# The causal mask of the transposed attention scores, added by VectorE in PSUM in place of a product with the identity on TensorE

## What is computed

```
mod = silu(c) @ wmod                      # six rows of 1024 per batch: sa, ca, ga, sb, cb, gb
h = layernorm(x) * (1 + ca) + sa
q, k, v = rope(h @ Wq), rope(h @ Wk), h @ Wv     # 32 query heads, 8 key/value heads, 32 wide
att = q . k / sqrt(32), -inf where key > query   # causal
x = x + ga * ((softmax(att) @ v) @ Wo)
h = layernorm(x) * (1 + cb) + sb
x = x + gb * (h @ W.T + bias + lora(h))
```

## Time and profile before

| what | us |
|---|---|
| median of 3 runs (2609.54 to 2612.29) | 2611.24 |
| profiled execution | 2611.64 |
| its span, first to last instruction | 2609.9 |
| PE busy / PEld busy | 2514.4 (96%) / 1871.7 (72%) |
| POOL busy | 1649.7 (63%) |
| DVE busy | 1577.4 (60%) |
| ACT busy | 1021.0 (39%) |
| granted TensorE clock, mean of the span | 0.973 |

### The profile page before, as it was taken

How to read it: one execution, slowest core, us unless ns; L and a number is a source line. 1 busy time by engine, 2 the same in 40 slices (tenths; PEclk the granted TensorE clock), 3 DMA queues, 4 the chain that set the end, 5 groups by cost and what they waited for, 6 DMA issues and landing times. The chain is left out here.

```text
span 2609.9 us, 37478 instructions
## 1 busy us (share of the span) xinstructions
PE 2514.4 (96%) x14476; PEld 1871.7 (72%) x14476; DVE 1577.4 (60%) x2509; ACT 1021.0 (39%) x1301; POOL 1649.7 (63%) x863
## 2 busy tenths in 40 slices
PE   5999999996999999999999999899899999999998
PEld 2788888885766666666666666565588788888886
DVE  4667666655766666666666666465755455454553
ACT  3333333321455665565555666465411111111110
POOL 4543333331488898988988889787555455555553
PEclk8999999997799999999999999899999999999999
DMA  7432233325324335225332335230433433333330
GB/s 277 137 114 103 99 114 113 113 89 173 95 74 131 79 81 139 76 67 144 83 91 53 71 81 161 56 79 19 161 97 97 111 91 97 108 95 105 113 89 25
DMA packets 179726, 267.53 MB, mean 103 GB/s; under 512 B 20508, under 2 KB 113884, under 8 KB 178400
## 3 DMA queue, kind: packets, MB, share of 16 engines
q1 hardware_dynamic: 179552, 265.13, 34.5%
HBM read 183.22 MB, written 80.81 MB: 101 GB/s over the span
## 5 line engine op out<-in xcount | busy, mean ns | idle before, releaser
L927 POOL TENSOR_TENSOR p_sum<-p_sum,p_ring 128x1024 f32<-128x1024 f32 (+2 forms) x465 | 993.9, 2171 | 188.5 <-PE ctx_ps L997 170.4
L850 DVE TENSOR_REDUCE neg_max<-scores_q 128x1 f32<-128x512 f32 (+3 forms) x1216 | 740.6, 658 | 390.8 <-PE scores_q L983 226.5
L792 ACT ACTIVATE p_ring<-scores 128x1024 f32<-128x1024 f32 (+2 forms) x512 | 463.6, 918 | 250.4 <-PE scores L965 178.9
L979 PE MATMUL scores_q<-k_stack,q_stack 96*128 96x512 f32 (+3 forms) x1536 | 467.5, 381 | 0.4 <-DVE prefetched L892 0.4
L961 PE MATMUL scores<-q_stack,k_stack 98*128 98x512 f32 (+1 forms) x1216 | 417.4, 421 | 12.7 <-ACT p_ring L792 11.8
L469 POOL TENSOR_TENSOR roped_hilo<-roped_hilo 128x512 fp32r<-128x512 f32 x80 | 104.3, 1304 | 333.2 <-ACT roped_hilo L329 333.2
L961 PEld LDWEIGHTS scores<-q_stack,k_stack 98*128 98x128 f32 x1216 | 195.5, 192 | 166.1 <-issue 96.2
L979 PEld LDWEIGHTS scores_q<-k_stack,q_stack 96*128 96x128 f32 x1536 | 284.7, 198 | 38.1 <-DVE neg_max L850 4.2
L512 PE MATMUL proj_ps<-h_hi,w_hi 128*128 128x512 f32 x768 | 304.6, 397 | 1.6 <-POOL h_lo L462 1.6
L512 PE MATMUL proj_ps<-h_hi,w_lo 128*128 128x512 f32 x768 | 300.2, 391 | 0.0
L512 PE MATMUL proj_ps<-h_lo,w_hi 128*128 128x512 f32 x768 | 300.0, 391 | 0.0
(11 more groups left out here) (147 smaller groups left out, 3722.3 us busy)
## 6 DMA issues: line engine op xcount, KB each, us to landing
q_stack<-qk_t SPq DMA_DIRECT2D x96, 512.0 KB, 6.9
qk_t<-roped_hilo SPq DMA_DIRECT2D x80, 512.0 KB, 2.7
x_in<-in_L_attn_resid SPq DMA_DIRECT2D x32, 512.0 KB, 6.3
prefetched<-in_L_wmod SPq DMA_DIRECT2D x4, 4096.0 KB, 13.9
ctx_t<-ctx_raw SPq DMA_DIRECT2D x64, 256.0 KB, 4.5
prefetched<-ctx_t SPq DMA_DIRECT2D x31, 512.0 KB, 4.1
prefetched<-inv_t SPq DMA_DIRECT2D x124, 128.0 KB, 5.4
k_stack<-qk_t SPq DMA_DIRECT2D x96, 128.0 KB, 8.8
```

The source lines that it names most:

```text
L792: nc.scalar.activation(probs(n, u), src, ACT.Exp, scale=SM_SCALE).then_inc(s_ex.sem, 1)
L850: nc.vector.tensor_reduce(negm[:, lo // HALF, hs[0]:hs[-1] + 1, i:i + 1], src, AX.X, ALU.max, negate=True).then_inc(s_mx.sem, 1)
L927: nc.gpsimd.tensor_tensor(a, a, probs(n, u), ALU.add).then_inc(s_ap.sem, 1)
L979: last = nc.tensor.matmul(dst[:, a, :], qs[0:MHI, n % QS, h, i * P:(i + 1) * P], ks[0:MHI, n % QS, lo:lo + w], start=not first, stop=not d ...
```

## The change

The mask products on PE go, with the table `mask_k_q` and its four copies on ACT. In their place DVE adds the mask (third part of `consts`, in SBUF, repeated over the heads) to the first 128 columns of each head of a diagonal unit, in place in PSUM (`mask_diagonal`), at the step "scores" of its list: behind the maxima of the steps before it. The exponential of a diagonal unit waits for that add (`diagonal_masked`) instead of the scores; the others wait for the scores as before. The wait of PE and DVE at the start of the stage counts four copies fewer.

```diff
+DIAGONAL = [u for u in range(NE) if EXP_UNITS[u][3] == P * EXP_UNITS[u][1]]
+ND = len(DIAGONAL)
...
-        maskT = sb("mask_k_q", [P, G, P], F32R)
...
+        def scores_of(n, u):
+
+            w, t = EXP_UNITS[u][4], sc[(NE * n + u) % SS]
+            return (t[:, :].rearrange("p (h n) -> p h n", h=2)[:, :, 0:w] if w > 256
+                    else t[:, 0:G * w].rearrange("p (h n) -> p h n", h=G))
...
             def exp(n, u):
                 hf, j, hs, lo, w = EXP_UNITS[u]
-                act.wait_ge(s_p2.sem, s_p2.at(NE * n + u + 1))
+                if u in DIAGONAL:
+                    act.wait_ge(s_dm.sem, s_dm.at(ND * n + DIAGONAL.index(u) + 1))
+                else:
+                    act.wait_ge(s_p2.sem, s_p2.at(NE * n + u + 1))
...
+            def mask_diagonal(n, u):
+                at, heads = scores_of(n, u)[:, :, 0:P], len(EXP_UNITS[u][2])
+                dve.wait_ge(s_p2.sem, s_p2.at(NE * n + u + 1))
+                nc.vector.tensor_tensor(at, at, consts[:, 2 * P:3 * P].rearrange("p (a n) -> p a n", a=1).broadcast_to([P, heads, P]),
+                                        ALU.add).then_inc(s_dm.sem, 1)
...
-                if kind == "mod":
+                if kind == "scores" and step[2] in DIAGONAL:
+                    mask_diagonal(n, step[2])
+                elif kind == "mod":
...
-                                            qs[0:KS, n % QS, h0:h0 + per, lo:lo + w], start=True, stop=not diag)
-                if diag:
-                    for a in range(len(hs) // per):
-                        last = nc.tensor.matmul(o[a][:, :, 0:P], identr[:, :], maskT[:, 0:per, :], start=False, stop=True)
+                                            qs[0:KS, n % QS, h0:h0 + per, lo:lo + w], start=True, stop=True)
                 last.then_inc(s_p2.sem, 1)
```

More of the change, by code:

```diff
@@ L595, in attention @@
         s_mr = [count(f"max_stacked{i}", 32) for i in range(QS)]
-        s_p2, s_ex, s_pv = count("exp_scores"), count("probs_ready"), count("values_done")
+        s_p2, s_ex, s_pv, s_dm = count("exp_scores"), count("probs_ready"), count("values_done"), count("diagonal_masked")
         s_av, s_ap = count("probs_added_dve"), count("probs_added_pool")
@@ L770, in _ @@
                 nc.scalar.activation(maskS[:, h, :], consts[:, P:2 * P], ACT.Copy).then_inc(init.sem, 1)
-                nc.scalar.activation(maskT[:, h, :], consts[:, 2 * P:3 * P], ACT.Copy).then_inc(init.sem, 1)
             def exp(n, u):
                 hf, j, hs, lo, w = EXP_UNITS[u]
-                act.wait_ge(s_p2.sem, s_p2.at(NE * n + u + 1))
+                if u in DIAGONAL:
+                    act.wait_ge(s_dm.sem, s_dm.at(ND * n + DIAGONAL.index(u) + 1))
+                else:
+                    act.wait_ge(s_p2.sem, s_p2.at(NE * n + u + 1))
                 if j == 0:
@@ L788, in exp @@
                             act.wait_ge(s_ap.sem, s_ap.at(NP * before[0] + POOL_ADDS.index(before[1]) + 1))
[L789 to L792, removed]
+                nc.scalar.activation(probs(n, u), scores_of(n, u), ACT.Exp, scale=SM_SCALE).then_inc(s_ex.sem, 1)
             def take_ctx(n, hf):
@@ L841, in _ @@
             nc.vector.memset(negm[:, 1, :, 0:WIDE[0]], LARGE).then_inc(init.sem, 1)
-            dve.wait_ge(init.sem, 2 * G + 5)
+            dve.wait_ge(init.sem, G + 5)
             def take_max(n, m):
@@ L945, in _ @@
         def _(pe):
-            pe.wait_ge(init.sem, 2 * G + 5)
+            pe.wait_ge(init.sem, G + 5)
             def scores(n, u):
@@ L954, in scores @@
                     pe.wait_ge(s_ex.sem, s_ex.at(at - SS + 1))
-                diag = lo == P * j
                 per = 1 if w > 256 else HALF // w
```

## The result

The changed kernel takes 2575.71 us (median of 4 runs, 2574.49 to 2579.28) against 2611.76 before (4 runs, 2609.54 to 2613.45): ratio 0.9865, 95% interval 0.9848 to 0.9882. The forecast was 2580, the range 2551 to 2614.

What follows compares the result with a forecast made beforehand. PE was taken as the bound at 35.48 us a group; minus 2.32 removed, plus stalls of 0.56 and 0.68, gives 34.40. 31 × 1.08 saved less 2 in the last group: 2611.6 − 31.5 = 2580 us, range 2551 to 2614.

Steps and rivals of the forecast that it cites:

- PE is the bound before: Ordinary attention group: PE issues without a pause and sets the 35.48 us period; POOL is second, 3.4 us short of it.
- Removed: 2.32 us: PE, per group: dropping 22 mask products saves 2.32 us by their starts, so PE alone would need 33.16 us.
- the 2.2 below which the prediction called itself wrong: Sign of error: PE's starts next to the removed products move by less than 2.2 us per group.
- Price of the add: VectorE: 12 mask adds per group, eight at 0.43 and four at 0.69 us, 6.2 us in all.
- The walk, 0.56 + 0.68 = 1.24: Units 2 to 5 and 16 to 19 traced: PE stalls 0.56 us at unit 5 and 0.68 at units 18 and 19.
- Hidden: POOL and the copy of the maxima: Per group: POOL's adds have 1.99 us of slack; the maxima copy lands 0.4 us before the next unit 0; neither cuts in.
- POOL's floor: POOL's adds keep the period from going under 33.54 us; rival with POOL setting the pace: 2553 us, chance 0.17.
- Last group, +2 (0 to 5): Last attention group: masks may queue behind 15 VectorE adds, one or two waits costing 2 us, 0 to 5.
- The sum, 33.5 saved and 2 given back: Whole kernel: 31 groups at 1.08 us save 33.5, the last group gives back 2, leaving 31.5 saved.
- The rival "slower": VectorE's queue takes PE's place: 0.1 us more per mask costs 0.5 us a group; 2637 us at 0.8; chance 0.15.

Runs made afterwards that it cites:

- the kernel without masks: Against the kernel before: mask of the transposed scores left out on both engines, exponential scale 1/16 of the real one; 2543.75 us, ratio 0.9751.
- moving mask 3: Against the changed kernel: on VectorE the mask of unit 3 put ahead of the one maximum reduction just before it; 2580.9 us, period 34.53.
- relieving the queue behind mask 3: Against the changed kernel: the mask of unit 4 alone back on PE, all others on VectorE; 2578.05 us, period 34.42.
- a mixed placement: Against the changed kernel: masks of units 3 and 17 and of the whole last group back on PE, elsewhere on VectorE; 2560.13 us, period 33.85.

## Why the prediction was right, step by step

- **PE is the bound before.** Held, except in units 5 and 17: the period falls in every run that removes products, leaves the maximum units in place and gives VectorE no more than the masks once (33.50 to 35.04).
- **Removed: 2.32 us.** Measured 35.47 − 33.34 = 2.13, just under the 2.2 below which the prediction called itself wrong, and differently made. A pair of products is mostly worth 0.22, not 0.17: the step looked at the product before the pair, which keeps its length, and not at the one behind. The two max products behind mask 3 took 1440.50 − 1439.98 = 0.52 us before and 1446.79 − 1446.32 = 0.47 after. In units 5 and 17 nothing is saved, because a wait for reductions takes the time back: in the kernel without masks the second max product of unit 5 starts 0.36 us after the first (0.23 before), and in unit 17 the product that transposes the maxima 0.27 after its neighbour (0.10 before). Without mask delays and without POOL the period is 33.34, not 33.16.
- **Price of the add.** 0.43 and 0.69 taken, 0.426 and 0.691 measured.
- **The walk, 0.56 + 0.68 = 1.24.** Measured against PE's own 33.34: 34.43 − 33.34 = 1.09. By the columns it is 0.70 before unit 5, less 0.13 that unit 5's own stretch gives back, 0.34 and 0.14 in the stretches of 18 and 19 (0.38 and 0.30 forecast), and 0.06 in those of 1 and 3. The mechanism at unit 5 is shown twice: moving mask 3 moves exp 3, relieving the queue behind mask 3 moves nothing. Removal 0.19 too large and stalls 0.15 too large cancel; that the period came out only 0.03 off is partly luck.
- **Hidden: POOL and the copy of the maxima.** POOL's floor was 33.54 forecast, 33.50 measured, and not reached. The copy landed 0.41 us before unit 0 where 0.4 was forecast.
- **Last group, +2 (0 to 5).** 6.3 measured in and behind it: the scores' 1.9 was priced, the 4.4 behind them was not. Of these, 3.8 are the sum that waits for the delayed adds; the other 0.6 lie behind the sum, where the granted share of the clock was 0.59 instead of 0.72. Masks on PE there take both back.
- **Not priced: group 0.** It saved 3.7 us, not 1.08 (39.40 to 35.72). It begins at the lower of the two clock levels, 1.2 GHz, and goes to 2.4 GHz after 13.7 us in the kernel before and after 10.1 us in the changed one (granted share 0.50 up to 682.50 and 679.00, then 1.00, PE busy all the time); over the whole group the share is 0.826 and 0.858. By these shares 6.9 and 5.1 us of full clock were lost (39.40 × 0.174, 35.72 × 0.142). So an estimate of 1.8 of the 2.6 us is the clock. The run with the last group's masks on PE agrees: its group 0 has the changed kernel's work and a share of 0.827, by which it should be 1.3 us longer; it is 1.27. Why the clock rose earlier in the changed kernel was not tested.
- **The sum, 33.5 saved and 2 given back.** The traces have 37.1 and 6.3, and 6.5 more saved in the linear stage, of which the prediction said that it moves forward whole. Errors of +3.6 (2.6 of it group 0, the rest, net, groups with a modulation product), −4.3 and +6.5 us stand against each other: the attention stage alone saved 30.8 where 31.5 was forecast, and that closeness is in part luck. By the medians 36.05 us were saved, 4.5 more than forecast; by the traces these come from the linear stage, and why is open.
- **The rival "slower".** Its slope was too mild: 0.5 us a group per 0.1 us of mask was forecast; 3.04 us for twelve times 0.34 to 0.60 is 0.7 to 0.9. With it, an estimate that takes the slope as even, the gain is gone at a mask about 0.12 to 0.15 us dearer, not 0.22: the forecast stood nearer to its edge than it said.

## What to carry to other kernels

Moving work off the engine that sets the pace gives what that engine's starts say, less the delay the work now adds where it sticks out over the cover; find those places unit by unit, for they were three of twelve here. Keep the old way exactly there (a mixed placement, with the last group on PE, won 15.6 us more), and look for the waits right behind the first one, such as three banks in rotation, before reordering. Price the last group by itself: there another job stands in the queue of the engine that receives the work.

## What was not expected of the hardware

- A pair of 128-column products, each with its own weight load, takes 0.17 us from start to start, and the 512-column product behind it 0.29 instead of 0.23 (0.573 to 0.859 in unit 3 before, 0.401 to 0.632 without masks, medians from the unit's start). Short products cost a little more than their own starts say; what takes the 0.05 was not tested.
- A stage that no edit touches differs by 17 us among the traces of fourteen kernels (728.9 to 745.7), with stalls of PE at the turns of its loop in seven of them, for which the profile names no releaser. The runs of one kernel agree much better (before: 2604.6 to 2613.5 us over all its runs), so this may well belong to the kernel and not to the execution; with one trace of each kernel that is not shown.
